# One matrix instead of two, transposing loads in the GRU passes, straight programs instead of loops

## The chip, the core and the metric

The kernel runs on one NeuronCore of a Trainium2 chip. The metric is device time in microseconds for one launch. The engines are PE (TensorE matmuls; PEld its weight loads), DVE (VectorE), ACT (ScalarE), POOL (GpSimd) and SP (SyncE, which only issues DMAs here). Sixteen DMA engines serve the core.

## The reference, cut to what matters

A graph of 12,500 nodes and 200,000 edges runs through four graph networks, one after the other, with a layer norm after each. In short:

```
L0: two hops; per edge a message of 64 numbers in hyperbolic space, summed at the edge's dst, divided by its count
L1: two GRU steps; m = segment_sum(W @ [h_dst, h_src, edge_weight]) ; h = GRU(m, h)
L2: SAGE conv 64 -> 16 -> 64 (two sums over neighbours)
L3: SAGE conv 64 -> 128 -> 64 (two sums over neighbours)
```

L0 works on edges. L1 to L3 need six plain sums over neighbours. They are computed as dense products with an adjacency matrix A of counts (12,544 x 12,544 in fp16, about 315 MB): A x for the last four, and the same with A transposed for the first two, the GRU passes.

## The kernel before, in words

A block is 128 nodes; there are NB = 98. The matrix is split in two halves by node block (54 and 50 blocks wide, four in both), so that two streams of scatters can run into each half.

Stages, in order of time; all five engines meet after each:

- **Ranking** (`rank`, `degrees`): edges are sorted by block. POOL scatters them in bursts of 40 DMAs (line 734) and DVE and PE compute the places for the next burst. Meanwhile SP fills the matrix with zeros (line 497).
- **Building the matrix** (`list_keys`, `find_same`, `find_edges`): for each of 52 groups of 32 tiles of 128 edges, DVE finds duplicates and makes addresses. POOL adds each tile's counts into `adj` with one indirect DMA (line 749), 1,664 in all, in four streams. Each stream waits for its own last DMA. In `find_same` (line 1920) DVE compares `keys_on` with `ekey`, in `find_edges` (line 1930) `srcf` or `dstf` with `heavy_on`. All of these lie in SBUF. Nodes with over 2,048 edges have a side path, the heavy rows.
- **Two edge passes** (L0, `run_pass(0)` and `(1)`): POOL gathers 32 tiles in a burst (line 762), DVE computes messages, PE fetches heads (line 1026) and sums.
- **Six dense passes** (`run_dense(2)` to `(7)`). A pass goes over the matrix in sweeps of up to 8 blocks of destination nodes. In a sweep SP loads units of at most 1 MB into a ring of four buffers, PE multiplies each 128x128 block (as weights) with 192 columns of x in three bf16 parts (line 1121), and DVE adds the three parts at the sweep's end (line 2254).

The matrix exists twice. `adj` has the far node as its row, `back` the near node. Passes 2 and 3 (`ALONG`, 14 sweeps of 26 units of 4 far blocks, 1,024 columns wide) read `adj`. Pass 3 also writes `back`. For each block PE makes a second matmul with the identity (line 1118), ACT and DVE copy the turned blocks from PSUM to SBUF (lines 1333 and 2266), and SP stores them (line 596). Passes 4 to 7 (`AGAINST`, 13 sweeps of 28 units) read `back`. GRU and convolution stages stand between the passes.

Repeated work is written with `Fori` loops. In them a wait on a semaphore goes by a register, and `await_reg` adds one increment of a `tick` semaphore behind it. The ordering within an engine is the order of the program; between engines semaphores alone order.

Of the kernel before, what the change touches and what calls it, by code (L numbers as in the profile page):

```python
# [20 lines left out]
I32 = mybir.dt.int32  # L21
# [6 lines left out]
P = 128  # L28
# [7 lines left out]
G = 32  # L36
# [44 lines left out]
ADJ_ROWS = NB + 1  # L81
BACK_ROWS = (COLS[0], COLS[1] + 1)
SOURCES = NB + 3
FAR = float(2 ** 30)
PAD_KEY = -4.0e6
D3 = 3 * D
# [3 lines left out]
def in_units(k, n):  # L90

    short = UK * n - k
    sizes = [UK] * (n - short) + [UK - 1] * short
    assert sum(sizes) == k and 0 <= short <= n
    return [(sum(sizes[:j]), sizes[j]) for j in range(n)]


class Shape:
# [3 lines left out]
    def __init__(self, units, stages):  # L102
        self.units = units
        self.stages = stages
        self.n = len(units)
        self.sweeps = sum(len(w) * t for _, _, w, t in stages)
        assert 2 * self.n % RING == 0 and self.n * self.sweeps % RING == 0

    def walk(self):

        before_ = 0
        for half_, c0, widths, turns in self.stages:
            yield half_, c0, widths, turns, before_
            before_ += len(widths) * turns


def far_sources(half_, k):

    if half_ == 0:
# [6 lines left out]
AGAINST = Shape([(v, k0, kn, [far_sources(v, k) for k in range(k0, k0 + kn)])  # L126
                 for v in range(2) for k0, kn in in_units(BACK_ROWS[v], 14)],
                [(None, 90, (8,), 1), (None, 0, (8, 7), 6)])
# [11 lines left out]
def build(nc, a, out):  # L140
    ctx = ExitStack()
    with ctx:
# [11 lines left out]
        adj_flat = [nc.dram_tensor(f"adj_{v}", (ADJ_ROWS * P * COLS[v] * P, 1), FP16, kind="Internal").ap() for v in range(2)]  # L154
        adj = [adj_flat[v].rearrange("(r c) k -> r (c k)", c=COLS[v] * P) for v in range(2)]
        back = [nc.dram_tensor(f"back_{v}", (BACK_ROWS[v] * P, NB * P), FP16, kind="Internal").ap() for v in range(2)]
# [142 lines left out]
        heavy_on = [flat_x[:, 1024 + P * k:1024 + P * k + P] for k in range(2)]  # L299
# [7 lines left out]
        heavy_near = flat_x[:, 2920:2920 + NB]  # L307
# [7 lines left out]
        ring = [v.bitcast(FP16).rearrange("p (k c) -> p k c", k=UK) for v in  # L315
                (side[:, 512:512 + UNIT_F], side[:, 512 + UNIT_F:512 + 2 * UNIT_F], flat_hot[:, 0:UNIT_F], flat_hot[:, UNIT_F:2 * UNIT_F])]
        turned_out = [flat_hot[:, (2 + k) * UNIT_F:(3 + k) * UNIT_F].bitcast(FP16) for k in range(2)]
# [3 lines left out]
        ident16 = flat_sc[:, 544:544 + P // 2].bitcast(FP16)  # L321
# [10 lines left out]
        ps_sort_iota = bank[2][:, 3 * P:4 * P]  # L332
        ps_degree = [bank[7][:, P * k:P * k + NB] for k in range(2)]
# [7 lines left out]
        tick = {k: sem(f"tick_{k}") for k in ("sp", "pool", "dve", "act", "pe")}  # L341
# [31 lines left out]
        turn_made, turn_act, turn_dve, out_act, out_dve = (sem(x) for x in ("turn_made", "turn_act", "turn_dve", "out_act", "out_dve"))  # L373
        out_stored = [sem(f"out_stored_{k}") for k in range(2)]
# [33 lines left out]
        def await_reg(eng, who, s, v):  # L408


            eng.wait_ge(s, v)
            eng.sem_inc(tick[who], 1)
# [9 lines left out]
        def units_before(m):  # L422

            return sum(v.n * v.sweeps for v in [ALONG] * min(m - 2, 2) + [AGAINST] * max(m - 4, 0))

        def sweeps_before(m):

            return sum(v.sweeps for v in [ALONG] * min(m - 2, 2) + [AGAINST] * max(m - 4, 0))
# [26 lines left out]
        lof, pad_, edge_a, edge_b, sum_s, sum_d, edge_not = (sc[:, 8 + k, :] for k in range(7))  # L455
# [5 lines left out]
        def _(sp):  # L461
# [12 lines left out]
            with sp.Fori(0, GROUPS) as g:  # L474
                sp.dma_start(pv[bass.ds(g, 1)].rearrange("a q t k -> (a q) t k"), fill).then_inc(filled, 16)
# [19 lines left out]
            for b in range(ADJ_ROWS):  # L495
                for v in range(2):
                    sp.dma_start(adj[v][P * b:P * b + P, :], zeros_dram[:, 0:COLS[v] * P]).then_inc(zeroed, 16)
# [16 lines left out]
            def load_hot(m, i, h, u, free):  # L514
                if free:

                    await_reg(sp, "sp", scattered, 4 * i + (m * SUMMED + 2 * h + u - 3))
                sp.dma_start(onehot[:, h, half(u), :].rearrange("p t n -> p (t n)"),
                             head_hots[bass.ds(4 * i + (2 * h + u), 1)].rearrange("a q c -> (a q) c")).then_inc(hot_moved[h][u], 16)
# [31 lines left out]
            def run_pass(m):  # L551
# [4 lines left out]
                with sp.Fori(1, ITERS) as i:  # L556
                    for h in range(2):

                        await_reg(sp, "sp", S["gathered", m][h], i * (G * 16))
                        await_reg(sp, "sp", hot_made, 4 * i + (m * HOT + 2 * h - 2))  # L560
                        load_pay(i, h)

                        await_reg(sp, "sp", S["coefficients", m], MIXES * 2 * i + MIXES * (h - 1))
# [7 lines left out]
            def run_dense(m):  # L571

                shape, turning = ALONG if m < 4 else AGAINST, m == 3
                mats = [v.rearrange("(k p) c -> p k c", p=P) for v in (adj if m < 4 else back)]
                done = units_before(m)

                def load_unit(half_, step, i, j, at, w):

                    v, k0, kn, _ = shape.units[j]
                    if i is None:  # L580
                        sp.wait_ge(unit_free, done + step + 1)
                    else:
                        await_reg(sp, "sp", unit_free, i * (2 * shape.n) + (done + step + 1))
                    r = (done + step) % RING
                    sp.dma_start(ring[r][:, 0:kn, 0:w * P], mats[half_ if v is None else v][:, k0:k0 + kn, at]).then_inc(unit_here[r], 16)

                def store_unit(half_, step, i, j, at, w):

                    _, k0, kn, _ = shape.units[j]
                    kn = min(kn, NB - k0)  # L590
                    for s in (out_act, out_dve):
                        if i is None:
                            sp.wait_ge(s, step + 1)
                        else:
                            await_reg(sp, "sp", s, i * (2 * shape.n) + (step + 1))
                    sp.dma_start(back[half_][at, P * k0:P * k0 + P * kn].rearrange("(c p) d -> p c d", p=P),
                                 turned_out[step % 2][:, 0:w * kn * P].rearrange("p (c d) -> p c d", c=w)).then_inc(out_stored[step % 2], 16)

                def store_x3():
                    sp.dma_start(table_lin.rearrange("(b p) c -> p b c", p=P), x3[:, 0:NB, :]).then_inc(x3_stored, 16)  # L600

                def stage_(half_, c0, widths, before_, i):

                    behind = []
                    for s, w in enumerate(widths):
                        c = P * (c0 + sum(widths[:s]))
                        at = slice(c, c + P * w) if i is None else bass.ds(i * (sum(widths) * P) + c, P * w)
                        for j in range(shape.n):
                            step = shape.n * (before_ + s) + j
                            load_unit(half_, step, i, j, at, w)  # L610
                            if step == RING - 1 and not turning:
                                store_x3()
                            if turning:
                                behind.append((half_, step, i, j, at, w))
                                if len(behind) > 2:
                                    store_unit(*behind.pop(0))
                    for unit in behind:
                        store_unit(*unit)

                if turning:  # L620
                    store_x3()
                for half_, c0, widths, turns, before_ in shape.walk():
                    if turns == 1:
                        stage_(half_, c0, widths, before_, None)
                    else:
                        with sp.Fori(0, turns) as i:
                            stage_(half_, c0, widths, before_, i)
                if turning:
                    for k in range(2):
                        sp.wait_ge(out_stored[k], (shape.n * shape.sweeps // 2 + 1) * 16)  # L630
                meet(sp, BN[f"pass{m}"])
# [7 lines left out]
            def store_steps(dst, srcv, s, before_):  # L639
                nonlocal stored  # L640
                v = dst.rearrange("(b p) c -> p b c", p=P)
                with sp.Fori(0, NITERS) as i:
                    await_reg(sp, "sp", s, i + (before_ + 1))
# [18 lines left out]
            sp.dma_start(adj[0][NB * P:NB * P + P, 0:LOW_TO * P], kept[:, 0:LOW_TO * P]).then_inc(stores, 16)  # L662
# [39 lines left out]
            for k in range(2):  # L702
                sp.sem_inc(out_stored[k], 16)
# [1803 lines left out]
```

## Time and profile before

| | |
|---|---|
| time, median of 3 runs | 22558.81 us (22556.67 to 22565.64) |
| the profiled execution's own time | 22546.55 us |
| its span | 22544.4 us |
| PE, DVE, ACT, POOL busy | 56%, 38%, 13%, 37% |
| DMA, mean | 159 GB/s |
| matrix building | 3357.6 to 6996 us |
| pass 2 (reads `adj`) | 14675 to 15642 us |
| pass 3 (reads `adj`, writes `back`) | 15845 to 17868 us |

Busy shares are means over stages with different limits, so the stages have to be read one by one. A row of an engine's waits says who was waited for, the total in us, how often, and the longest.

### The profile page before, as it was taken

The numbers are of one execution on the slowest core, as the hardware profiler recorded it, in microseconds if no ns is written. First come the engines' busy times: TensorE is split into PE (matmuls) and PEld (weight loads), VectorE is DVE, ScalarE is ACT, GpSimd is POOL, SyncE is SP. The second block draws the span as 40 slices with busy tenths as digits, with TensorE's granted clock in tenths as the row PEclk, the third lists the DMA queues.
The fourth block names the chain that finished last, engine by engine and source line by source line (L and its number), as shares of the span: only waits on it lengthen the run. The fifth ranks groups of instructions, "written<-read, shape, count | busy, mean of one in ns | idle before, by whom it ended". The sixth has DMA issues, their size and how long they took to land. (4 is left out here: it accounts for less than half of the span.)

```text
span 22544.4 us, 302048 instructions
## 1 busy us (share of the span) xinstructions
PE 12710.9 (56%) x103818; PEld 11283.5 (50%) x103819; DVE 8510.4 (38%) x15488; ACT 2879.7 (13%) x5263; POOL 8346.1 (37%) x6810
## 2 busy tenths in 40 slices
PE   2222225333322555555555555488777788878887
PEld 1111114333322444444444444388677687878787
DVE  4444446444442555555455555501434400010101
ACT  0000000000001222222122222100343300000000
POOL 4444447888886555554455555300000000000000
PEclk6555556555555555555555555599999999999998
DMA  9600014333332222222222222297899697989798
GB/s 358 272 1 1 1 32 111 77 77 77 77 71 45 71 69 72 71 71 62 69 70 70 70 71 71 54 339 271 297 334 340 236 336 273 316 294 347 263 322 305
DMA packets 2131032, 3586.46 MB, mean 159 GB/s; under 512 B 554444, under 2 KB 1429728, under 8 KB 2037429
## 3 DMA queue, kind: packets, MB, share of 16 engines
q1 hardware_dynamic: 1732405, 3389.59, 42.5%
q0 software_dynamic: 397504, 181.65, 6.6%
q8 instruction: 735, 12.04, 0.2%
q14 instruction: 388, 3.18, 0.0%
HBM read 2672.91 MB, written 907.26 MB: 159 GB/s over the span
## 5 line engine op out<-in xcount | busy, mean ns | idle before, releaser
L762 POOL DMA_INDIRECT room<-table_hyp,pay x3328 | 3430.5, 1031 | 1116.5 <-issue 984.3
L1026 PE MATMUL pair<-room,side 128*128 x6656 | 1688.3, 435 | 2973.9 <-ACT side L1354 2432.6
L1121 PE MATMUL pair<-room,side 128*128 128x192 bf16 x30694 | 3049.1, 250 | 508.0 <-DMA side<-back 327.1
L749 POOL DMA_INDIRECT adj<-sc x1664 | 2962.8, 1781 | 791.9 <-issue 485.3
L1026 PEld LDWEIGHTS pair<-room,side 128*128 128x128 f32 x6656 | 1480.7, 327 | 3287.6 <-issue 3287.6
L1121 PE MATMUL pair<-room,onehot 128*128 128x192 bf16 x31058 | 3006.1, 247 | 110.4 <-DMA onehot<-back 74.8
L1121 PEld LDWEIGHTS pair<-room,side 128*128 128x128 f16 x30694 | 2664.5, 100 | 593.3 <-issue 453.8
L1121 PEld LDWEIGHTS pair<-room,onehot 128*128 128x128 f16 x31058 | 2629.1, 98 | 193.7 <-issue 138.1
L791 POOL DMA_INDIRECT sc<-table_lin,heavy_idx x6 | 5.7, 950 | 6957.4 <-DMA table_lin<-room 6957.4
L734 POOL DMA_INDIRECT payload<-room x1600 | 1554.9, 972 | 1685.7 <-DVEq L1706 1094.9
L2254 DVE TENSOR_REDUCE acc<-pair 128x384 f32 (+2 forms) x314 | 145.3, 526 | 4300.0 <-PE pair L1121 4296.7
L2266 DVE CAST onehot<-pair 128x512 f16<-128x512 f32 (+2 forms) x1372 | 816.6, 613 | 1153.5 <-PE pair L1118 861.7
L1017 PE MATMUL pair<-ident,onehot 128*128 128x128 f32 x3328 | 860.0, 421 | 412.0 <-DMA onehot<-head_hots 412.0
L2146 DVE TENSOR_TENSOR side<-pay,pair 128x512 f32<-128x512 int32 x208 | 142.0, 683 | 2499.1 <-remote 2491.7
L1354 ACT COPY side<-pair 128x512 f32<-128x512 f32 x832 | 477.6, 586 | 4174.5 <-remote 3522.3
L1333 ACT CAST onehot<-pair 128x512 f16<-128x512 f32 x1372 | 775.1, 587 | 1256.3 <-PE pair L1118 913.6
L1017 PEld LDWEIGHTS pair<-ident,onehot 128*128 128x128 f32 x3328 | 721.0, 240 | 412.3 <-issue 412.3
L1118 PE MATMUL pair<-sc,onehot 128*128 128x128 f16 x5090 | 749.4, 221 | 235.5 <-DVE onehot L2266 142.6
L1118 PE MATMUL pair<-sc,side 128*128 128x128 f16 x5102 | 752.6, 222 | 205.8 <-DVE onehot L2266 116.5
L907 PE MATMUL pair<-ident,sc 128*32 128x128 f32 x52 | 20.6, 396 | 1420.7 <-DVEq L1891 1420.7
L837 PE MATMUL pair<-onehot,xs 125*128 125x98 bf16 x1600 | 210.7, 270 | 1075.1 <-issue 1048.5
L1066 PEld LDWEIGHTS pair<-xs,onehot 128*128 128x128 f32 x3328 | 717.6, 332 | 137.7 <-issue 137.7
(437 smaller groups left out, 18105.7 us busy)
## 6 DMA issues: line engine op xcount, KB each, us to landing
onehot<-back SPq DMA_DIRECT2D x308, 1024.0 KB, 7.7
side<-back SPq DMA_DIRECT2D x280, 1024.0 KB, 7.7
onehot<-back SPq DMA_DIRECT2D x264, 896.0 KB, 7.1
side<-back SPq DMA_DIRECT2D x240, 896.0 KB, 7.3
onehot<-head_hots SPq DMA_DIRECT2D x208, 1024.0 KB
adj<-xs SPq DMA_DIRECT2D x99, 1728.0 KB
adj<-xs SPq DMA_DIRECT2D x99, 1600.0 KB
side<-adj SPq DMA_DIRECT2D x148, 1024.0 KB, 8.6
```

The lines of the kernel that those rows point to most:

```text
L734: pool.indirect_dma_start(out=payload[:, :], out_offset=bass.IndirectOffsetOnAxis(ap=addr[:, h, c:c + 1], axis=0), in_=stage[:, h, c, :], ...
L749: pool.indirect_dma_start(out=adj_flat[q // 2][:, :], out_offset=bass.IndirectOffsetOnAxis(ap=edge_to[i % 2][q][:, t:t + 1], axis=0), in_= ...
L762: pool.indirect_dma_start(out=rows[:, h, t, :], out_offset=None, in_=table_hyp[:, :], in_offset=bass.IndirectOffsetOnAxis(ap=pay[:, h, t, ...
L837: last = nc.tensor.matmul(ps_degree[k], key_[:, c, :], blk_[:, h, c, :], start=first and c == 0, stop=False, skip_group_check=True)
L1017: last = nc.tensor.transpose(ps_sel[q % 2][:, j * P:j * P + P], onehot[:, h, 4 * q + j, :], ident[:, :])
L1026: last = nc.tensor.matmul(ps_head[:, j * TW:j * TW + TW], sel_t[:, q % 2, j * P:j * P + P], flat_tab[:, bass.ds(b * TW, TW)], start=True, ...
L1066: last = nc.tensor.matmul(sums[:, bass.ds(at, D)], onehot[:, h, t, :], head[h][:, t, 0:D], start=False, stop=False, skip_group_check=True)
L1118: flip = nc.tensor.matmul(o[:, P * (c % 4):P * (c % 4) + P], block_, ident16, start=True, stop=True)
L1121: last = nc.tensor.matmul(banks[c // 2][:, D3 * (c % 2):D3 * (c % 2) + D3], block_, x3[:, sources[k], :], start=j + k == 0 and c % 2 == 0, ...
L1333: nc.scalar.copy(o[:, 0:4, k, :], v[:, :].rearrange("p (c d) -> p c d", c=4)).then_inc(turn_act, 1)
L1354: nc.scalar.copy(sel_t[:, q % 2, :], ps_sel[q % 2][:, :]).then_inc(sel_copied, 1)
L2266: V.tensor_copy(o[:, 4:w, k, :], v[:, 0:(w - 4) * P].rearrange("p (c d) -> p c d", d=P)).then_inc(turn_dve, 1)
```

## The change

1. The matrix is kept once, as `mat`, with the near node as row. It has the layout that `back` had. POOL adds the counts straight into it. `back`, the turning in pass 3 (PE's second matmuls, the copies by ACT and DVE, the stores) and `adj` are gone. The zeroes go to `mat`, about as many bytes as before, in 208 DMAs and two small ones.
2. Passes 2 and 3 need the far node on the partitions. SP therefore loads them with `dma_start_transpose`. A unit is now 512 rows (4 near blocks) by 8 far blocks, whose rows give pieces of 2 KB, in 13 units and 27 sweeps: 351 units a pass. The heavy rows come from a small array `heavy_near`, one more plain load in each sweep's last unit.
3. In the matrix building, DVE copies each group's keys to PSUM (`ps_own_keys`) and `heavy_on` is left in PSUM, so that lines 1920 and 1930 read one operand from PSUM. The address arithmetic has a few more small instructions.
4. Every `Fori` becomes a Python loop, so each program is straight; `await_reg` becomes a plain wait on a constant, and the `tick` increments go.

The diff, cut to its core (the loops and waits of point 4 are changed everywhere in the same way):

```diff
-ALONG = Shape([(None, k0, kn, list(range(k0, k0 + kn))) for k0, kn in in_units(ADJ_ROWS, 26)],
-              [(1, 42, (8,), 1), (1, 0, (7, 7), 3), (0, 48, (6,), 1), (0, 0, (8, 8), 3)])
+ALONG = Shape([(None, k0, kn, list(range(k0, k0 + kn))) for k0, kn in in_units(NB + 1, 13, 2 * UK)],
+              [(v, c, min(UM // 2, COLS[v] - c)) for v in (1, 0) for c in range(0, COLS[v], UM // 2)])
...
-        adj_flat = [nc.dram_tensor(f"adj_{v}", (ADJ_ROWS * P * COLS[v] * P, 1), FP16, kind="Internal").ap() for v in range(2)]
-        back = [nc.dram_tensor(f"back_{v}", (BACK_ROWS[v] * P, NB * P), FP16, kind="Internal").ap() for v in range(2)]
+        mat_flat = [nc.dram_tensor(f"mat_{v}", (MAT_ROWS[v] * P * NB * P, 1), FP16, kind="Internal").ap() for v in range(2)]
+        heavy_near = [nc.dram_tensor(f"heavy_near_{v}", (P, COLS[v] * P), FP16, kind="Internal").ap() for v in range(2)]
...
+        heavy_on = [bank[2][:, P * k:P * k + P] for k in range(2)]
+        ps_own_keys = [bank[2][:, 2 * P + G * h:2 * P + G * h + G] for h in range(2)]
...
-        def await_reg(eng, who, s, v):
-            eng.wait_ge(s, v)
-            eng.sem_inc(tick[who], 1)
+        def until(eng, s, v):
+            if v > 0:
+                eng.wait_ge(s, v)
...
+                    if v is None:
+                        sp.dma_start_transpose(ring[shape][r][:, 0:far, 0:w * P], mat[half_][near, P * k0:P * k0 + P * far]).then_inc(unit_here[r], 16)
...
+                    if far < kn:
+                        sp.dma_start(ring[shape][r][:, far, 0:w * P], heavy_near[half_][:, near]).then_inc(unit_here[r], 16)
...
-                                if flips:
-                                    o = bank[4 + 2 * ((k0 + k) % 2) + c // 4]
-                                    flip = nc.tensor.matmul(o[:, P * (c % 4):P * (c % 4) + P], block_, ident16, start=True, stop=True)
...
+                V.tensor_copy(ps_own_keys[h], ekey[h])
...
-                stt(a_, dstf[h], float(COLS[n % STREAMS // 2]), tile_colf[:, tiles_], ALU.mult, ALU.add)
+                V.tensor_scalar(far_block, far_, 7, None, ALU.arith_shift_right)
+                V.tensor_scalar(b_, far_, P - 1, None, ALU.bitwise_and)
+                dve.drain()
+                stt(edge_row, tile_colf[:, tiles_], float(P), a_, ALU.mult, ALU.add)
+                stt(a_, edge_row, float(NB), far_block, ALU.mult, ALU.add)
...
-                V.tensor_tensor(same[h], keys_on[h].rearrange("p (t e) -> p t e", e=P), over(ekey[h], P), ALU.is_equal)
+                V.tensor_tensor(same[h], keys_on[h].rearrange("p (t e) -> p t e", e=P), over(ps_own_keys[h], P), ALU.is_equal)
```

## Rows read from the trace of the kernel before

**Rows 1.** Busy time by stage: us, then each engine's busy us, PE clock, DMA share, GB/s.

```profile
core 0: us, PE busy (x) PEld busy (x) DVE busy (x) ACT busy (x) POOL busy (x), PEclk, DMA share, GB/s
3357.60:6996.00 3638.40, 1334.95 (x7788) 1151.78 (x7788) 1590.59 (x1313) 224.05 (x550) 2962.79 (x1664) 0.55 0.38 76
7000.00:10750.00 3750.00, 2036.02 (x8535) 1771.39 (x8535) 1945.55 (x5011) 802.81 (x1365) 1911.09 (x1768) 0.50 0.24 69
14675.00:15642.00 967.00, 886.56 (x10298) 851.42 (x10298) 25.98 (x60) 0.00 (x0) 0.97 (x1) 0.98 1.00 354
15845.00:17868.00 2023.00, 1553.33 (x20490) 1446.16 (x20490) 844.98 (x1440) 775.07 (x1372) 0.96 (x1) 0.96 0.98 335
18101.00:19040.00 939.00, 873.47 (x10164) 841.55 (x10164) 25.39 (x57) 0.00 (x0) 0.00 (x0) 0.98 1.00 355
```

**Rows 2.** Groups of instructions by line, the scatter of the matrix building.

```profile
L749 POOL DMA_INDIRECT adj<-sc x1664 | 2962.8, 1781 | 791.9 <-issue 485.3 <-DVEq L1945 215.6 <-DMA adj<-sc 91.0
```

**Rows 3.** Timeline of the matrix building: start us, us, engine, line, operation.

```profile
4013.71 0.18 DVE L1539 TENSOR_SCALAR sc<-sc 128x32 int32<-128x32 int32 x1
4013.77 1.54 POOL L749 DMA_INDIRECT adj<-sc  x1 [0.30 <-issue]
4014.77 4.43 DVE L1920 TENSOR_TENSOR room<-room,sc 128x4096 bf16<-128x4096 f32 x1
4015.62 4.99 POOL L749 DMA_INDIRECT adj<-sc  x1 [0.30 <-issue]
4020.72 2.29 DVE L1912 TENSOR_TENSOR side<-pay,pair 128x2048 f32<-128x2048 int32 x1 [0.19 <-issue]
4020.91 1.54 POOL L749 DMA_INDIRECT adj<-sc  x1 [0.31 <-issue]
...
4025.60 8.76 DVE L1930 TENSOR_TENSOR onehot<-sc,xs 128x4096 bf16<-128x4096 f32 x2
4029.03 2.42 POOL L749 DMA_INDIRECT adj<-sc  x1 [2.88 <-DMA adj<-sc]
```

**Rows 4.** Waits in the matrix building, 3360 to 7000 us.

```profile
DVE sc L1941 <- DMA adj<-sc: 1541.2, 11, 145.1
DVE pair L2175 <- POOLq L405: 391.0, 1, 391.0
```

**Rows 5.** Groups of instructions by line, the turning of pass 3.

```profile
L1118 PE MATMUL pair<-sc,onehot 128*128 128x128 f16 x5090 | 749.4, 221 | 235.5 <-DVE onehot L2266 142.6
L1118 PE MATMUL pair<-sc,side 128*128 128x128 f16 x5102 | 752.6, 222 | 205.8 <-DVE onehot L2266 116.5
L2266 DVE CAST onehot<-pair 128x512 f16<-128x512 f32 (+2 forms) x1372 | 816.6, 613 | 1153.5 <-PE pair L1118 861.7
L1333 ACT CAST onehot<-pair 128x512 f16<-128x512 f32 x1372 | 775.1, 587 | 1256.3 <-PE pair L1118 913.6
```

**Rows 6.** DMA by queue, pass 2, 14700 to 15600 us: packets, MB, engine share.

```profile
q1 hardware_dynamic: 173953, 319.01, 99.6%
```

**Rows 7.** DMA by queue, pass 3, 15900 to 17800 us.

```profile
q1 hardware_dynamic: 507381, 636.20, 97.7%
```

**Rows 8.** DMA by queue in the ranking stage, 1000 to 3300 us.

```profile
q0 software_dynamic: 36768, 2.39, 1.7%
```

**Rows 9.** Timeline of pass 4, PE alone.

```profile
18310.49 7.36 PE L1121 MATMUL pair<-room,side 128*128 128x192 bf16 x64 [5.80 <-issue]
18317.68 5.44 PE L1121 MATMUL pair<-room,onehot 128*128 128x192 bf16 x64
```

**Rows 10.** Timeline of the ranking stage: the first two rows straight, then in a loop.

```profile
115.36 5.49 DVE L1709 TENSOR_TENSOR head<-room,pair 125x5120 bf16<-125x5120 int32 x1 [0.23 <-issue]
189.65 5.49 DVE L1709 TENSOR_TENSOR head<-room,pair 125x5120 bf16<-125x5120 int32 x1 [0.23 <-issue]
...
2033.96 5.49 DVE L1709 TENSOR_TENSOR head<-room,pair 125x5120 bf16<-125x5120 int32 x1 [0.23 <-issue]
...
2107.95 5.49 DVE L1709 TENSOR_TENSOR head<-room,pair 125x5120 bf16<-125x5120 int32 x1 [0.23 <-issue]
```

**Rows 11.** Waits in edge pass 0, 7500 to 10500 us.

```profile
DVE side L2146 <- remote: 1054.3, 42, 27.1
POOL rel L772 <- DVEq L2127: 513.9, 21, 24.7
DVE sc L2006 <- issue: 40.5, 42, 4.5
```

More of the change, by code:

```diff
@@ L98, with __init__ @@
 class Shape:
-    def __init__(self, units, stages):
+    def __init__(self, units, sweeps):
         self.units = units
-        self.stages = stages
+        self.sweeps = sweeps
         self.n = len(units)
[L106 to L114, printed above, removed]
 def far_sources(half_, k):
@@ L599, in store_x3 @@
[L599 to L630, printed above, removed]
+                shape, done = ALONG if m < 4 else AGAINST, units_before(m)
@@ L776, in run_pass @@
                 gather(m, 0, 1)
-                with pool.Fori(0, ITERS - 1) as i:
+                for i in range(0, ITERS - 1):
                     for h in range(2):
@@ L975, in _ @@
                     degrees(k, 0, h, h + k == 0)
-            with pe.Fori(1, NITERS + 1) as i:
+            for i in range(1, NITERS + 1):
                 for h in range(2):
@@ L981, in _ @@
                 q_step(i - 1)
-            with pe.Fori(NITERS + 1, GITERS) as i:
+            for i in range(NITERS + 1, GITERS):
                 for h in range(2):
@@ L1072, in run_pass @@
                 fetch_group(m, 0, 0)
-                with pe.Fori(0, ITERS - 1) as i:
+                for i in range(0, ITERS - 1):
                     fetch_group(m, i, 1)
@@ L1179, in gru @@
                 gates(0, 0, False)
-                with pe.Fori(0, NITERS // 2 - 1) as i:
+                for i in range(0, NITERS // 2 - 1):
                     for h in range(2):
@@ L1223, in conv @@
                 second_layer(0, 0, False)
[L1224 removed]
+                for i in range(0, NITERS // 2 - 2):
                     for h in range(2):
@@ L1395, in run_pass @@
                     pass
-                with act.Fori(0, ITERS - 1) as i:
+                for i in range(0, ITERS - 1):
                     group(2 * i, 0, steps(2 * i + 1, 1))
@@ L1468, in gru @@
                 turned(1, 1)
-                with act.Fori(0, NITERS // 2 - 1) as i:
+                for i in range(0, NITERS // 2 - 1):
                     for h in range(2):
@@ L1501, in conv @@
                 hidden(1, 1, False)
-                with act.Fori(0, NITERS // 2 - 2) as i:
+                for i in range(0, NITERS // 2 - 2):
                     for h in range(2):
@@ L1795, in make_q @@
             def make_q():
-                with dve.Fori(0, NITERS) as i:
+                for i in range(0, NITERS):
                     keep_q(i, 1)
@@ L1801, in _ @@
             rsum(relblk[:, :, D], rel_sq)
-            with dve.Fori(1, NITERS + 1) as i:
+            for i in range(1, NITERS + 1):
                 for h in range(2):
@@ L1811, in _ @@
             dve.drain().then_inc(table_ready, 1)
-            with dve.Fori(NITERS + 1, GITERS) as i:
+            for i in range(NITERS + 1, GITERS):
                 for h in range(2):
```

358 lines of the change are left out of this document (136 added, 222 removed).

## Prediction

> **What bounds the kernel now.** The kernel is a string of stages that end in a meeting of all engines, so I read the busy time by stage first. The matrix building lasts 3638 us, and POOL is busy for 2963 of them; pass 2 lasts 967 us at a DMA share of 1.00, pass 3 2023 us at 0.98, pass 4 939 us at 1.00 [rows 1]. Passes 2 and 4 thus go at the pace of the DMA engines, with PE close behind (887 of 967 us). Pass 3 moves the matrix twice, in and out, and that is its length. Then I read who waits at the end of the matrix building: DVE stands for 391 us at the meeting until POOL comes, and on the way it waited 1541 us for the scatters that POOL issues [rows 4]. POOL sets the end there. Then the groups by line and the timeline, for what POOL's time consists of.
>
> **1. Matrix building: one operand moves to PSUM.** The scatter of line 749 takes 1.54 us, but its mean over 1,664 is 1.781 us [rows 2, 3]. The timeline shows where the rest comes from. A scatter that meets DVE's line 1920 (both operands in SBUF, 4.43 us) takes 4.99 us, one that meets the pair of line 1930 is late as well, while one beside line 1912 (as wide a comparison by column, one operand in PSUM) takes 1.54 us [rows 3]. The change gives both slow lines the form of line 1912. The excess is 2962.8 - 1664 x 1.543 = 395 us, all on POOL's path. Of the 91 us that POOL waited for its own scatters to land [rows 2] some follow from a scatter issued late; the one in [rows 3] stands behind line 1930. I take 35 of 91. The 485 us of issue, 0.30 each, stay. Gain: 430 us, bounds 0 (if the PSUM operand does not free POOL) and 395 + 91 = 486 us.
>
> What is late next? DVE: it gets a copy, a shift, a drain and a multiply-add more, under 1 us for each of 52 groups at the 0.18 us of such an instruction [rows 3]. It has 1541 + 391 us of waiting to hide 50 in [rows 4]. The new rows of the matrix put a tile's 128 counts on 128 rows instead of 128 other rows; I count nothing.
>
> **2. Passes 2 and 3: transposing loads.** Removed from pass 3: 10,192 identity matmuls, 1,372 copies each on ACT and DVE [rows 5], and the stores, half of what the DMAs carry. What stays is a pass with the matmuls of pass 2 whose loads transpose. No row shows such a load, so I bound it by packets.
>
> A packet's price follows from two stretches. In pass 2, 900 us x 16 x 0.996 / 173,953 = 82.4 ns for 1,834 B on average [rows 6]; in pass 3, 1,900 x 16 x 0.977 / 507,381 = 58.5 ns for 1,254 B [rows 7]. The line through both is 6.8 ns + 0.0412 ns per byte. The ranking's scatters, 65 B on average, took 2,300 x 16 x 0.017 / 36,768 = 17 ns [rows 8] where the line says 9.5, so tiny pieces can be dearer.
>
> A pass loads 104 near x 98 far blocks of 32 KB, 334 MB, and some 10 us of heavy rows. If the transposing load costs what its source pieces of 2 KB cost, the pass is pass 2 or 4 again: 939 to 967 us. If its price is that of 1 KB pieces (512 rows x 2 B is what each partition gets), 334 MB / 1,024 x 49.0 ns / 16 = 999, with the heavy rows 1,010 us. If it is broken into 256 B, the row of one 128x128 block, 334 MB / 256 x 17.4 / 16 = 1,419, so 1,430 us. At 128 B with the 17 ns of [rows 8] it is 2,772, so 2,780 us; at 32 B (16 rows of one partition) with that price, 11,100 us, which I name as the far end.
>
> I take 1,260 us: the middle of 1,010 and 1,430 is 1,220, and pass 2 at 967 was 3% over the best plain pass at 939. That is an estimate. Both passes: 2 x 1,260 - (967 + 2,023) = -470 us, ends -1,110 and some thousands above. Loading, not PE, is then the bound: a unit of 32 matmuls is 32 x 85 ns = 2.7 us (64 in 5.44 us [rows 9]) and comes every 3.6 us, 75% busy. Pass 3 was 77% busy and its granted clock was 0.96, the 2.4 GHz level [rows 1], so I leave the clock there.
>
> The Trainium skill, "DMA: Bandwidth & Descriptors", section "Latency and other measured facts", gives a transposing DMA 261 GB/s where short pieces cannot be joined to 4 KB, and 350 to 400 where they can. By its 261, an estimate from the page, a pass is 334 / 0.261 = 1,280 us and the whole some 40 us above my sum. The same skill, "Advanced Engine Details and Errata", section "X-Bar Transpose (TRN2)", says that such DMAs are as fast as regular ones; that is the first rival. Against the change speaks "VectorE: DVE Perf Modes", section "The three transpose paths": 1.309 us for one 128x128 block through the DMA. If blocks went one at a time at that price, a pass would be 10,192 x 1.309 = 13,300 us, the whole some 46,000. No row here shows any of the three.
>
> **3. Straight programs.** Passes 4 to 7 show 5 turns of a loop each with 5 to 7 us of issue before PE's first matmul, 5.80 us in [rows 9]. The pass moves at the DMA's pace with share 1.00 in spite of them [rows 1]: the ring of four runs full while PE stands, and PE at 2.7 us a unit catches up. I count nothing; if the cover failed, four passes would gain 4 x 5 x 5.5 = 110 us. In the ranking the same piece of work recurs after 74.3 us where it is straight already and after 74.0 us inside the loop [rows 10]: nothing. In the edge passes POOL's burst and the part of DVE's work that it waits for (24.5 us a group) follow one another [rows 11]; DVE's issue gaps at the head of a group are 1 us each, 40.5 us in 42 groups [rows 11], and a straight wait on a constant may save a third. Over 104 groups: 40 us, bounds -50 (if fetching each instruction once, where a loop kept them, costs half a microsecond a group) and 150.
>
> **Sum.** From the profiled execution, 22546.55 us (span 22544.4): -430 - 470 - 40 = -940, so 21,607. The median shown is 12 us above that execution, so 21,620.
>
> **Rivals.**
> - *As fast as a plain load.* Both passes at 950 us: -1,090, and -430 - 40: 20,987 + 12, or 21,000. For it: nothing but the pieces of 2 KB, the same that pass 2 reads. Against: each partition receives 2 B of a row at a time.
> - *Small pieces decide, slower than before.* The write side of the transposing load, or SP making its descriptors, costs by pieces of 128 B or less. At 128 B and 17 ns: 2 x 2,780 - 2,990 = +2,570, less 470: 24,660. It decides from the point where both passes eat all gains, (2,990 + 470) / 2 = 1,730 us a pass, 4.9 us a unit against the 2.9 of a plain one. For it: the price per packet rises fast under 512 B, and a transposition must split rows somewhere. Against: nothing in the trace.
> - *The PSUM operand frees nothing.* POOL stays at 1.781 us: 22,050. Against it stands line 1912 in [rows 3].
> - *PE falls to 1.2 GHz in the starved passes.* The edge passes have PE 54% busy and a granted clock of 0.50 [rows 1]. At half clock a unit is 5.4 us of matmuls, a pass 1,900 us: 2 x 1,900 - 2,990 - 470 gives 22,890. Against it: pass 3 at 77% kept 0.96.
>
> **Chances.** Forecast 0.47; plain speed 0.17; small pieces 0.28 (0.02 of it for blocks one at a time); nothing freed 0.05; clock 0.03. The likeliest one's own range is 21,150 to 22,050, from its two piece sizes and the bounds of step 3. The range for 8 in 10 must reach the plain load below (20,950 with the small terms' bounds) and the 128 B case above (24,700); what lies beyond is mostly the far end of the small pieces. Within 0.2%, about what a measurement of this kernel can tell from no change, lies only a pass near 1,730 us: 0.03. Slower takes nearly all of the small pieces and of the clock: 0.29. Faster: 0.68.
>
> **What would show it.** Step 1: line 749 at a mean near 1.55 us and a building stage of some 3,200 us. Step 2: passes 2 and 3 equally long; their length divided by 351 is the price of a unit, and the DMA packets' sizes tell which piece sets it; if the DMA share is low while PE waits, SP's issue is the limit instead. Step 3: passes 4 to 7 unchanged within 1%, edge passes within 1%. The prediction is wrong if a unit takes over 4.9 us, or if the building stage keeps its 3,638 us.

## The result, and the profile after

The kernel after the change takes 21301.62 us (median of 4 runs, 21295.46 to 21308.47), the kernel before 22562.22 us in the same job. The ratio is 0.9442, with a 95% interval of 0.9425 to 0.9458. 21,620 us had been predicted: the sign and the size are right, but an error of 650 us too much gain and one of 970 us too little cancel in the sum. That it came so near is in part luck.

The stages, read off the timelines of POOL and PE (us; "to the scatter" is from the start to the first scatter of counts, "building" from there to the first gather, "edge" from the first to the last gather, "pass 2" and "pass 3" from the first to the last product, "from pass 4" to the span's end). The span also holds the gaps between them, 71 us shorter after the change. All kernels of the experiments stand here too:

```
kernel             to the scatter  building   edge  pass 2  pass 3  from pass 4    span
before                       3358      3643   7466     966    1998         4471   22544
after                        3277      3401   6835    1456    1461         4293   21294
b_psum                       3371      3398   7513     962    1996         4468   22342
b_straight                   3289      3646   6877     934    1930         4306   21577
b_straight_psum              3295      3393   6891     939    1935         4300   21352
b_straight_ticks             3338      3648   7499     941    2000         4322   22369
b_waits_apart                3320      3645   7180     939    1957         4315   21972
b_ticks_act                  3298      3636   7021     938    1945         4292   21741
b_ticks_pe                   3300      3650   7111     942    1992         4307   21914
a_plain                      3295      3395   6902     919     924         4298   20306
a_lag                        3297      3397   6904    1457    1457         4295   21380
a_1024x4                     3275      3400   6835    1444    1444         4301   21275
a_store                      3276      3397   6840    2185    1003         4305   21582
a_pause                      3271      3404   6436    1399    1396         4302   20785
```

The edge passes of a_plain last 6902 us and those of the kernel after 6835, though the edit of a_plain does not touch them. So a difference of up to some 70 us between two runs of this table tells nothing by itself.

The edge passes gave 631 us, half of the whole gain, where 40 us of all straight programs had been forecast. Busy time by stage after the change (us, each engine's busy us, PE clock, DMA share, GB/s) answers to [rows 1]:

```profile
3277.40:6673.00 3395.60, 1339.38 (x7788) 1151.47 (x7788) 1623.82 (x1513) 224.78 (x550) 2568.21 (x1664) 0.56 0.42 82
7000.00:10750.00 3750.00, 2017.99 (x9416) 1771.44 (x9416) 2088.33 (x5384) 870.80 (x1478) 2060.83 (x1902) 0.56 0.26 76
13800.00:15100.00 1300.00, 901.77 (x9307) 831.32 (x9306) 24.11 (x48) 0.00 (x0) 0.00 (x0) 0.93 1.13 235
15500.00:16700.00 1200.00, 808.68 (x8567) 744.09 (x8568) 22.07 (x44) 0.00 (x0) 0.00 (x0) 0.95 1.13 235
17001.00:17939.00 938.00, 879.48 (x10290) 841.07 (x10291) 23.62 (x53) 0.00 (x0) 0.94 (x1) 0.99 1.03 365
```

In the same 3,750 us of edge pass POOL issues 1,902 instructions instead of 1,768, and is as busy per instruction. Passes 2 and 3 are equally long now. Their DMA share is above 1, yet only 235 GB/s move, where a plain pass moves 365. The groups of the scatter and of the gather, after:

```profile
L724 POOL DMA_INDIRECT room<-table_hyp,pay x3328 | 3442.3, 1034 | 1114.8 <-issue 983.3 <-DVEq L2088 112.0 <-DMA pay<-payload 5.0
L711 POOL DMA_INDIRECT mat<-sc x1664 | 2568.6, 1544 | 943.0 <-issue 488.9 <-DMA mat<-sc 240.4 <-DVEq L1859 213.8
```

A scatter takes 1.544 us on average instead of the 1.781 of [rows 2]. But POOL waits 240 us for its own scatters to land, where it waited 91.

### The profile page after: what moved, and what is told of

Read it like the earlier page. It is cut to its first block and busy times, and to the rows that moved or that the text cites. A ratio compares the mean times of both kernels' runs of the same rounds, so it can differ in the third digit from the quotient of the medians.

```text
span 21293.8 us, 239475 instructions
## 1 busy us (share of the span) xinstructions
PE 11816.1 (55%) x93626; PEld 10393.3 (49%) x93626; DVE 7720.3 (36%) x14316; ACT 2087.3 (10%) x3871; POOL 7963.9 (37%) x6810
## 5 line engine op out<-in xcount | busy, mean ns | idle before, releaser
L1068 PE MATMUL pair<-room,onehot 128*128 128x192 bf16 x30652 | 2772.8, 252 | 835.1 <-DMA onehot<-mat 801.0
L1068 PE MATMUL pair<-room,side 128*128 128x192 bf16 x31100 | 2797.1, 250 | 551.8 <-DMA side<-mat 511.9
L988 PE MATMUL pair<-room,side 128*128 x6656 | 1414.9, 380 | 2787.9 <-issue 1811.0
L711 POOL DMA_INDIRECT mat<-sc x1664 | 2568.6, 1544 | 943.0 <-issue 488.9
L988 PEld LDWEIGHTS pair<-room,side 128*128 128x128 f32 x6656 | 1235.6, 278 | 3020.9 <-issue 3020.9
L2157 DVE TENSOR_REDUCE acc<-pair 128x128 f32<-128x384 f32 (+1 forms) x308 | 147.0, 532 | 5974.9 <-PE pair L1068 5974.9
L799 PEld LDWEIGHTS pair<-onehot,xs 125*128 125x128 bf16 x1600 | 143.2, 126 | 1557.1 <-issue 1393.2
L1028 PE MATMUL pair<-xs,onehot 128*128 128x64 f32 x3328 | 737.2, 423 | 48.2 <-ACT xs L1301 48.2
L1028 PEld LDWEIGHTS pair<-head,onehot 128*128 128x128 f32 x3328 | 717.6, 332 | 86.8 <-issue 86.8
L1028 PE MATMUL pair<-head,onehot 128*128 128x64 f32 x3328 | 737.2, 423 | 0.0
```

The source lines that it names most:

```text
L711: pool.indirect_dma_start(out=mat_flat[q // 2][:, :], out_offset=bass.IndirectOffsetOnAxis(ap=edge_to[i % 2][q][:, t:t + 1], axis=0), in_= ...
L799: last = nc.tensor.matmul(ps_degree[k], key_[:, c, :], blk_[:, h, c, :], start=first and c == 0, stop=False, skip_group_check=True)
L988: last = nc.tensor.matmul(ps_head[:, j * TW:j * TW + TW], sel_t[:, q % 2, j * P:j * P + P], flat_tab[:, bass.ds(b * TW, TW)], start=True, ...
L1028: last = nc.tensor.matmul(sums[:, bass.ds(at, D)], onehot[:, h, t, :], head[h][:, t, 0:D], start=False, stop=False, skip_group_check=True)
L1068: last = nc.tensor.matmul(banks[c // 2][:, D3 * (c % 2):D3 * (c % 2) + D3], block_, x3[:, sources[k], :], start=j + k == 0 and c % 2 == 0, ...
L2157: V.reduce_sum(o, v, axis=AX.X)
```

## Experiments

Names in `b_` start from the kernel before, in `a_` from the kernel after. Each is given as a ratio to the kernel before in its own job; that one measured from 22531 to 22602 us over the jobs.

**b_psum: the PSUM operands alone.**

```diff
-        heavy_on = [flat_x[:, 1024 + P * k:1024 + P * k + P] for k in range(2)]
+        heavy_on = [bank[2][:, P * k:P * k + P] for k in range(2)]
+        ps_own_keys = [bank[2][:, 2 * P + G * h:2 * P + G * h + G] for h in range(2)]
...
+                V.tensor_copy(ps_own_keys[h], ekey[h])
...
-over(ekey[h], P), ALU.is_equal)
+over(ps_own_keys[h], P), ALU.is_equal)
```

> The kernel before with the two PSUM operands alone (the group's keys and the heavy nodes' row); loops, matrices and addresses as before. Theory (the SBUF operands made POOL's scatters dear, and the new layout took back part of the gain): scatters at a mean of 1.55 us instead of 1.78, building stage 3638 - 395 = 3240 us or a little less, in all 22150 to 22200. Rival (a faster stream of scatters must wait for its own landings whatever the layout): building stage some 3395 us as after the change, POOL's waits for its own DMAs some 240 us, in all 22320.

Measured: 22357.52 us, ratio 0.9895 (0.9879 to 0.9912), so 239 us less. The group of its scatters:

```profile
L750 POOL DMA_INDIRECT adj<-sc x1664 | 2570.3, 1545 | 939.0 <-issue 479.0 <-DMA adj<-sc 244.9 <-DVEq L1947 215.2
```

The layout is the old one, and the wait for landings is 244.9 us all the same. The rival holds: a faster stream waits for its own landings. The excess of 395 us is gone and 154 of it come back as that wait. The new row order costs nothing that was measured: the building stage lasts 3398 us here and 3401 in the kernel after.

**b_straight and b_straight_ticks: straight programs, without and with the tick increments.** Every `with eng.Fori(a, b) as i` becomes `for i in range(a, b)`, and the wait becomes, in the one and in the other:

```diff
             eng.wait_ge(s, v)
-            eng.sem_inc(tick[who], 1)      # removed in b_straight, kept in b_straight_ticks
```

> The kernel before with every loop unrolled, waits on constants and no tick increments; nothing else changed. Theory (straight programs alone shorten the edge passes and the dense ones): first gather to last gather of the edge passes falls from 7466 us to some 6835, passes 4 to 7 with their convolutions from 4472 to some 4295, start to first scatter from 3358 to some 3280; in all 22560 - 890 = 21670. Rival (the edge passes gain from something else, such as the place of buffers or the matrix's layout): they keep 7466 us, and the kernel stays between 22250 and 22560, which is what the prediction on record said of this step (40 us).

> The kernel before with every loop unrolled and waits on constants, but with the increment of a tick semaphore kept behind each of these waits. Theory (the register waits, branches and address arithmetic of the loops cost the time): as without the increments, 21670 us. Rival (the increments cost it, by holding up the engines that wait while POOL's burst fills the semaphore path): the edge passes keep 7466 us or most of it, and the kernel is at 22300 or more.

Measured: 21587.95 us, ratio 0.9555 (0.9539 to 0.9571), and 22396.77 us, ratio 0.9913 (0.9896 to 0.9929). So straight programs and waits without an increment give 1,009 us, and with the increments kept 800 of them are lost: 622 in the edge passes, the rest before the scatters, in pass 3 and in gaps. The rival of the second expectation is right. What the loops themselves cost is 200 us, nearly all from pass 2 on. Waits of DVE and POOL from 7500 to 10500 us, first without ticks, then with them, answer to [rows 11]:

```profile
DVE side L2148 <- remote: 430.6, 36, 19.0
POOL xs L774 <- DVEq L2129: 439.9, 23, 37.8
POOL rel L774 <- DVEq L2129: 397.1, 22, 19.9
DVE sc L2056 <- issue: 152.1, 44, 4.4
```

```profile
DVE side L2147 <- remote: 1099.6, 41, 27.5
POOL xs L773 <- DVEq L2128: 507.6, 21, 24.9
POOL rel L773 <- DVEq L2128: 504.1, 21, 24.8
```

With ticks DVE waits up to 27 us for an increment that PE makes, and POOL 5 to 6 us longer in each group for DVE. The first row of each fence is DVE's wait for `scattered`, the increment that PE makes behind its sums; it is shown at the next instruction, that of `make_half_hot`. The last row of the first fence is idle time of DVE itself, for which the profile shows no other engine. Before the change the longest entry of this kind was the 40.5 us of [rows 11].

**b_straight_psum: both.** It combines the two edits above.

> The kernel before, straight and without tick increments, and with the two PSUM operands; two matrices, the turning in pass 3 and plain loads stay. So it is the kernel after the change less its one matrix and its transposing loads. If the parts add up, 22597 - 1009 - 239 = 21350 us, and the one matrix with transposing loads is worth nothing or a few tens of us (after: ratio 0.9442, 21336 on the same scale). Rival: the parts do not add (PSUM operands make PE or the fetching slower once programs are straight), 21450 or more, and the transposing loads are a gain of 100 or more.

Measured: 21352.12 us, ratio 0.9446 (0.9430 to 0.9462). The parts add up (21,349 from the two alone). This is the kernel after the change without its one matrix and its transposing loads, and the kernel after has the ratio 0.9442. So that part of the change, forecast at -470 us, is worth nothing that was measured: passes 2 and 3 together last 2917 us after the change and 2874 here.

**b_waits_apart, b_ticks_act, b_ticks_pe: what of a tick costs.** Straight programs in each; behind the wait stands:

```diff
+            eng.wait_ge(s, v)              # b_waits_apart: met already, increments nothing
...
+            if who == "act":               # b_ticks_act; "pe" in b_ticks_pe
+                eng.sem_inc(tick[who], 1)
```

> The kernel before, straight, with each tick increment replaced by a second wait for the same constant, which is met already. That keeps an instruction of its own for the wait, but increments nothing. Theory (the increments cost the time, by the path that they share with the increments which other engines wait for): 21590 us, as without ticks. Rival (an instruction of its own for each wait costs it, whatever it increments): 22400, as with ticks.

> The kernel before, straight, with the tick increments kept on ACT alone (22 of the 68 of a group of an edge pass). Theory (a path that all engines share is what the increments fill): it costs about a third of the 800 us, so 21850. Rival (an increment holds up only its own engine, and ACT has time to spare): 21590 to 21650.

> The kernel before, straight, with the tick increments kept on PE alone (27 of the 68 of a group of an edge pass). With them on ACT alone (22) the edge passes lasted 144 us longer, with all 68 they lasted 622 longer. Theory (the cost goes by the number of increments, whichever engine makes them): 622 x 27 / 68 = 250 us or a little less, 21830. Rival (PE's are the costly ones, since PE stands in the middle of each group's chain): 400 us or more, 22000.

Measured: 21970.10 us (0.972, 0.9701 to 0.974), 21737.42 us (0.9617, 0.9598 to 0.9636) and 21896.93 us (0.9709, 0.9690 to 0.9729). A wait without an increment is mostly merged with the next instruction; with a second wait or a tick it becomes an instruction of its own (in the records of the trace PE has 415 semaphore instructions from 7500 to 10500 us without ticks, 1,176 with them, 1,236 with second waits). The second wait makes as many instructions in each group as the tick, and costs 303 of the 622 us in the edge passes. So the truth lies between theory and rival: about half goes to instructions of their own, about half to increments. By engine, 22 of the 68 ticks of a group (ACT) cost 144 us, 27 (PE) cost 234, all 68 cost 622: 0.06, 0.08 and 0.09 us for each tick in 104 groups. With the 70 us by which edge passes differ between runs, the cost goes roughly by their number, also on ACT, which has time to spare. These sums hold the instruction of its own as well.

**a_plain: passes 2 and 3 without the transposition.** The blocks arrive untransposed, so this kernel doesn't compute the GRU passes' sums.

```diff
-sp.dma_start_transpose(ring[shape][r][:, 0:far, 0:w * P], mat[half_][near, P * k0:P * k0 + P * far])
+sp.dma_start(ring[shape][r].rearrange("p k c -> p (k c)")[:, 0:w * far * P].rearrange("p (b c) -> p b c", b=w),
+             mat[half_][near, P * k0:P * k0 + P * far].rearrange("(b p) c -> p b c", p=P))
```

> The kernel after the change, with the transposing loads of passes 2 and 3 replaced by plain loads of the same 512 rows and 2 KB pieces; the blocks then arrive untransposed, so the transposition is left out of what is computed. Theory (the transposing load costs 256 B packets or SP's time for it, 4.13 us a unit): each pass falls from 1455 us to 940 to 967, the kernel by some 980 to 20320. Rival (351 smaller sweeps' worth of work on PE or the waits between units set the pass, not the transposition): passes 2 and 3 stay above 1200 us each, the kernel above 20800.

Measured: 20290.35 us, ratio 0.8977 (0.8962 to 0.8992). The passes last 919 and 924 us. The same bytes, pieces, sweeps and matmuls, only not transposed, take 537 us less in each pass: that is the price of transposing in the DMA. No other limit holds a pass above 924 us.

**a_1024x4: the units' shape.**

```diff
-in_units(NB + 1, 13, 2 * UK)],
-              [(v, c, min(UM // 2, COLS[v] - c)) for v in (1, 0) for c in range(0, COLS[v], UM // 2)])
+in_units(NB + 1, 26, UK)],
+              [(1, 42, 8)] + [(1, 7 * c, 7) for c in range(6)] + [(0, 48, 6)] + [(0, 8 * c, 8) for c in range(6)])
```

> The kernel after the change with the shape of unit that the loads had before: 1024 rows by 4 far blocks, 14 sweeps of 26 units, so each source row gives 1 KB instead of 2 KB. Theory (the transposing load costs by its 256 B packets, or by SP's time for them, whatever the length of the source rows): a pass stays at 1455 us (364 units x 4.1 less the narrower ones = 1455), the kernel within 60 us of 21340. Rival (the source pieces set the price): 1 KB pieces cost more, a pass 1550 us or longer, the kernel 21530 or more.

Measured: 21278.10 us, ratio 0.9434 (0.9419 to 0.9450), passes of 1444 us each. Source rows of 1 KB cost no more than those of 2 KB. The DMA queue in 13800 to 15100 us (packets, MB, share of 16 engines), first of the kernel after, then with this shape:

```profile
q1 hardware_dynamic: 1191922, 304.81, 112.6%
```

```profile
q1 hardware_dynamic: 1198338, 306.75, 113.1%
```

Both have packets of 256 B (304.81 MB / 1,191,922), the row of one 128x128 block, whatever the unit's shape. Each took 1,300 us x 16 x 1.126 / 1,191,922 = 19.6 ns. The share is over 1 because packets of an engine overlap in the records; by elapsed time one packet per engine was done every 1,300 x 16 / 1,191,922 = 17.5 ns. Only these two shapes were tried.

**a_store: storing the transposed units for pass 3.**

```diff
+                            act.wait_ge(unit_here[step % RING], landed(step))
+                            act.dma_start(far_mat[half_][:, k0:k0 + far, P * c0:P * c0 + P * w],
+                                          ring[ALONG][step % RING][:, 0:far, 0:w * P]).then_inc(unit_kept[step % RING], 16)
...
+                    if m == 3:
+                        sp.dma_start(ring[shape][r][:, 0:far, 0:w * P], far_mat[half_][:, k0:k0 + far, near]).then_inc(unit_here[r], 16)
```

> The kernel after the change; in pass 2 ACT's queue also stores each landed, transposed unit to a second matrix with the far node as row, and pass 3 reads that with plain loads in 1 KB pieces. Theory (the DMA engines are the bound of the transposing load, 112% busy by their queue's share): the stores come on top, pass 2 lasts 1455 + 940 = 2400 us, pass 3 some 990, the kernel 21340 + 480 = 21820. Rival (SP's 4.13 us for each transposing load is the bound, and the DMA engines have room): pass 2 stays under 1700, pass 3 some 990, the kernel 21340 - 220 to 470 = 20870 to 21120, faster than both kernels.

Measured: 21581.68 us, ratio 0.9567 (0.9551 to 0.9583). Pass 2 lasts 2185 us, so the stores of 334 MB add 729 us to it; pass 3 lasts 1003. The two queues in 13800 to 15100 us, and before them SP's transposing loads in the kernel after and in this one (start us, us, engine, line):

```profile
14298.92 4.14 SPq L584 DMA_TRANSPOSE onehot<-mat  x1
14303.11 8.39 SPq L584 DMA_TRANSPOSE side<-mat  x2
```

```profile
14297.38 6.99 SPq L591 DMA_TRANSPOSE onehot<-mat  x1
14304.47 13.36 SPq L591 DMA_TRANSPOSE side<-mat  x2
```

```profile
q1 hardware_dynamic: 792269, 202.67, 74.4%
q10 hardware_dynamic: 205597, 200.70, 44.8%
```

SP is busy with such loads back to back in both, 4.2 us each there and 6.7 here, for the same work. So SP does not set the pace: its time for the same load grows when the stores share the DMA engines. The theory holds in the main. Of the 940 us expected for the stores some 210 are hidden: the shares of both queues sum to 119%, so 112.6% had left a little room.

**a_lag: gathers in chunks of 4, each chunk waiting for the chunk before the last.**

```diff
+                    part = S["gathered", m][h][t // CH_G % 2]
+                    if t >= 2 * CH_G and t % CH_G == 0:
+                        pool.wait_ge(part, 16 * (G // 2 * i + t // (2 * CH_G) * CH_G))
```

> The kernel after the change; POOL's burst of 32 gathers is issued in chunks of 4, and each chunk waits until the chunk before the last has landed (two semaphores in turn), so that at most 8 gathers are under way. In the trace of the change PE, ACT and DVE stand some 10 to 20 us in the second half of each burst. Theory (semaphore increments come late because too many gathers are under way): the standstills go, POOL's wait for DVE of some 19 us a group shrinks by 5 to 15 us, the edge passes last 6835 - 500 to 1500 us. Rival (increments are late because POOL issues at all, or the standstill costs nothing on POOL's path): the edge passes stay within 100 us of 6835, or are longer by the waits, 3 x 2 us a group at most, 600 us.

Measured: 21379.62 us, ratio 0.9457 (0.9441 to 0.9473); the edge passes last 6904 us. The gathers had landed before the waits, so POOL never paused: its longest gap before a gather in the waits from 7500 to 10500 us is 0.7 us. So never more than 8 gathers had been under way, and more than 8 cannot be the cause; whether fewer matter was not tested. The 70 us that the edge passes are longer are no effect of the edit, since those of a_plain are as long.

**a_pause: one real pause in a burst**, on top of a_1024x4:

```diff
+                    part = S["gathered", m][h][t // CH_G % 2]       # CH_G = 16
+                    if t == CH_G:
+                        pool.wait_ge(S["gathered", m][h][0], 16 * CH_G * (i + 1))
```

> The kernel after the change with units of 1024 rows by 4 blocks (21278 us by itself); in each burst of the edge passes POOL waits before its 17th gather until the first 16 have landed, some 2 us. In all traces DVE stops about 20 us after a burst's start, for 25 us with tick increments and for 12 us without, and goes on before or after the burst's end. Theory (PE's increments are held up when POOL has issued for 20 us without a break, and a break clears it): the standstills of DVE and PE go, and the edge passes last 6835 + 200 - 104 x 5 to 15 us, between 5500 and 6500. Rival (a short break clears nothing): DVE still stops at 20 us, the edge passes last 6835 to 7050, the kernel 21280 to 21490.

Measured: 20752.92 us, ratio 0.9209 (0.9193 to 0.9224). It beats both kernels. The edge passes last 6436 us, 399 less than in a_1024x4, near the small end of the gain that the theory gave. The other 90 us of the gain came in passes 2 and 3, which this edit does not touch: 245 GB/s move there and 237 in a_1024x4. This run was made on another chip than a_1024x4; whether that is the reason is not shown. Timelines show the edge passes' gain. First b_straight, where a burst of POOL began at 9531:

```profile
9544.75 7.09 PE L1068 MATMUL pair<-head,onehot 128*128 128x64 f32 x32
9551.63 1.91 PE L1019 MATMUL pair<-ident,onehot 128*128 128x128 f32 x8
9552.75 0.95 POOL L764 DMA_INDIRECT room<-table_hyp,pay  x1 [0.30 <-issue]
...
9564.18 0.69 DVE L2148 TENSOR_TENSOR side<-pay,pair 128x512 f32<-128x512 int32 x1 [13.16 <-remote]
...
9572.86 0.95 POOL L764 DMA_INDIRECT room<-table_hyp,pay  x1 [0.30 <-issue]
9575.41 0.59 ACT L1356 COPY side<-pair 128x512 f32<-128x512 f32 x1 [34.75 <-remote]
9576.25 2.03 PE L1028 MATMUL pair<-room,side 128*128 x8 [22.71 <-issue]
```

DVE stands 13 us, ACT and PE until the burst is over. DVE waits for PE's sums of line 1068, which ended at 9551.84, ACT for PE's transposes of line 1019, which ended at 9553.54. So the one increment is 12 us late and the other 22. With the tick increments the same place looks like this, at the end of the burst whose last gather begins at 9577.90:

```profile
9577.90 0.95 POOL L763 DMA_INDIRECT room<-table_hyp,pay  x1 [0.30 <-issue]
9582.78 0.69 DVE L2147 TENSOR_TENSOR side<-pay,pair 128x512 f32<-128x512 int32 x1 [26.77 <-remote]
9583.50 1.07 ACT L1355 COPY side<-pair 128x512 f32<-128x512 f32 x2 [36.34 <-remote]
```

And with the pause:

```profile
9546.30 0.95 POOL L729 DMA_INDIRECT room<-table_hyp,pay  x1 [0.30 <-issue]
9549.03 0.95 POOL L729 DMA_INDIRECT room<-table_hyp,pay  x1 [1.78 <-DMA room<-table_hyp,pay]
9549.89 0.69 DVE L2066 TENSOR_TENSOR side<-pay,pair 128x512 f32<-128x512 int32 x1 [5.59 <-remote]
...
9550.61 0.59 ACT L1269 COPY side<-pair 128x512 f32<-128x512 f32 x1 [16.39 <-remote]
```

POOL rests 1.78 us, and 0.9 us after it goes on DVE is released, then ACT and PE. The delay is shorter and not gone. From 7500 to 10500 us the waits with the pause are these, against 1224.1 us (65 times, up to 36.7) of ACT for "remote" and 446.2 us (39 times, up to 16.7) of DVE in the kernel after:

```profile
ACT side L1269 <- remote: 954.0, 107, 16.4
DVE side L2066 <- remote: 191.8, 44, 5.6
```

The waits for landings empty POOL's queue of gathers, too. So these runs do not tell whether the rest of POOL or the empty queue lets the increments through. The two semaphores in turn, which a_pause needs as well, stand in a_lag without a gain.

Over all bursts from 7500 to 13000 us (75 to 88 of them), DVE's longest wait for "remote" in a burst is on average 25.3 us before, 26.8 with ticks, 21.4 with ticks on PE, 19.8 with second waits, 15.8 with ticks on ACT, 12.0 in b_straight, 11.3 after the change and 4.4 with the pause. It begins some 20 us after the burst's start in every kernel. What changes is its end: 4 us after the burst's end before, 12 us ahead of it after.

## Why the prediction was right and wrong

**What bounds each stage** was read rightly: POOL in the building, the DMA engines in the dense passes. Of the edge passes the text had the chain, POOL's burst and then 24.5 us for DVE, but took DVE's part for work. DVE L2146 waiting 1054 us for "remote", 25 us a group, stood in [rows 11] and was not asked about. That row pointed at the gain, though it does not measure it: after the change the wait is 15 us a group shorter, the group only 6 us.

**Step 1** (forecast -430, measured -239 alone and -242 in the building). That a scatter beside a PSUM operand takes 1.54 us was right (mean 1.544), and the POOL time of 395 us went. The mis-sized term is the wait for landings: 35 of 91 us were to go, and instead 154 came on top (244.9 us in b_psum). So the building stage lasts 3,401 us, not "some 3,200". A stream's next scatter now comes after 4 x 1.84 us instead of 4 x 2.08, and that leaves less time for the landing of the last one. That it is the interval is argued and not shown; that the layout is innocent is shown.

**Step 2** (forecast -470, measured -47 in the two passes against the kernel before, of which straight programs alone give 100; -12 as what the other two steps leave of the whole). The step that failed is "the middle of 1,010 and 1,430 is 1,220". Of the piece sizes named, the 256 B of a block's row is what the trace shows, and its end, 1,430 us, is 2% under the 1,458 measured; the 17.4 ns of the line are the 17.5 of a_1024x4's section. Two candidates that exclude each other have no middle: one of the two had to be named. "Loading, not PE, is then the bound" is right, and so is PE at about three quarters busy (901.77 of 1,300 us, 69%) with a granted clock of 0.93, so mostly the 2.4 GHz level. The 939 us of pass 4, "the best plain pass", are a reading error: the window of [rows 1] begins at 18101 us, but PE's first product of the pass is at 18072.68, and from there the pass lasts 965 us, as long as pass 2:

```profile
18072.68 6.81 PE L1121 MATMUL pair<-room,side 128*128 128x192 bf16 x64 [79.26 <-DMA side<-back]
```

The Trainium skill, "Advanced Engine Details and Errata", section "X-Bar Transpose (TRN2)", makes such a DMA as fast as a regular one. By that rule the passes would be those of a_plain, 920 us; the trace has 1,458, and the measurement decides. The same skill, "DMA: Bandwidth & Descriptors", section "Latency and other measured facts", has 261 GB/s where short pieces cannot be joined. That is the nearer case, and 11% above the 235 GB/s of these rows.

**Step 3** (forecast -40, bounds -50 to 150; measured -1,009 alone). This is where the prediction was wrong. The step that failed is "a straight wait on a constant may save a third" of DVE's 1 us gaps: it looked at the instructions' own time. The cost was not there: each loop wait carried an increment of a tick semaphore and was an instruction of its own, and with both the increments that matter come later. This was 800 of the 1,009 us, the loops themselves 200. The bound was the nearest row of the wrong quantity. For the ranking stage, where nothing was counted, the stretch to the first scatter fell by 69 us; for passes 4 to 7, where nothing was counted and 110 was the most, it was 165 from pass 4 on (178 after the change) and 100 in passes 2 and 3. There the ring did not cover all of PE's gaps: passes 4 to 7 took 965, 967, 988 and 967 us before and 938, 938, 934 and 941 after, where "unchanged within 1%" was forecast. The edge passes, with the same sign, are 8% shorter.

**Sum.** -239 - 12 - 1,009 = -1,260 against -940 forecast. Steps 1 and 2 were too hopeful by 650, step 3 too cautious by 970. **Rivals:** plain speed, small pieces under 256 B, nothing freed by PSUM and the clock at 1.2 GHz throughout are all excluded by the trace after. The side on which it ended was never in danger: a unit takes 4.15 us, and 4.9 was the point from which it turns.

## What to carry to other kernels

Where an engine waits for "remote" or for "issue" over 10 us in every round, find out what else runs in that stretch before anything is priced by instruction: here it was POOL's burst of 32 indirect DMAs without a pause, and one pause of 1.8 us in its middle gave 399 us in 104 groups. An increment that nobody waits for and a wait in an instruction of its own are not free beside such a burst. And a transposing load like this one is to be priced by packets of 256 B, in both shapes of unit that were tried: 537 us more for 334 MB than a plain load.

## What the runs showed of the hardware

- In the second half of a burst of 32 indirect DMAs, 1.25 us apart, semaphore increments made by PE reach other engines 12 to 22 us late (in b_straight PE's sums end at 9551.84 and DVE goes on at 9564.18; PE's transposes end at 9553.54 and ACT goes on at 9575.41). A pause of 1.78 us of POOL lets the waiting ones through; later ones in the same burst are late again (PE's matmuls of line 994 end at 9553.49 and ACT goes on at 9562.00). Why they are late stays open: a_lag excludes only that more than 8 DMAs under way are needed. PE's increments are not all that suffers: DVE has idle stretches of its own there, of up to 4.4 us (152.1 us in 44 at line 2056 of b_straight).
- In these stretches an extra increment costs on average about 0.045 us (319 us / 7,072, over all engines), a wait in an instruction of its own 0.043 us (303 / 7,072). How this divides among the engines was not measured.
- A scatter by indirect DMA takes 1.54 us beside DVE reading one operand from PSUM and up to 4.99 us beside DVE reading both from SBUF ([rows 3]; mean 1.545 in b_psum).
- Stores of 1 KB pieces beside transposing loads hid 210 of 940 us, at a summed share of 119%. In that stretch PE was 60% busy (779.14 of 1,300 us), and its mean granted clock was 0.77 where it is 0.93 in the kernel after, so between the two levels.
